# A windowed-attention transformer behind a state-space block on one core: scores and values in one alternating run, copies and waits in another order, and a new ending

## What is computed

```python
for i in range(6):
    # attention: 16 heads of 64, windows of 32, each looks at itself and the window before
    q, k, v = split(shift_tokens(x) @ Wqkv[i]);  q, k = l2norm(q) * qs, l2norm(k) * ks   # then rotary with scale
    sim  = where(mask, -inf, q @ k2.T * 8)        # 32 x 64 for each window and head
    x    = softmax(sim) @ v2 @ Wo[i] + x
    # feed-forward
    xn = layernorm(shift_tokens(x)) * g + b
    a, gate = split(xn @ W1[i] + b1[i]);  x = (a * gelu(gate)) @ W2[i] + b2[i] + x
out = resid + gb * x
```

## Time and profile before

| | us |
|---|---|
| median of 3 runs | 2083.33 |
| lowest and highest | 2079.34, 2084.64 |
| the profiled execution | 2082.23 |
| its span, first to last instruction | 2080.4 |
| busy: TensorE, VectorE, ScalarE, GpSimd | 1992.2, 1520.1, 1383.3, 1227.6 |
| mean granted share of TensorE's clock | 0.975 |

### The profile page before, as it was taken

The page is one execution under the profiler, slowest core; times in us unless marked ns, Lnnn a source line. Parts: engine busy times, 40 slices in busy tenths (PEclk is TensorE's granted clock), DMA queues, the critical chain, the costliest instruction groups (busy, mean ns, idle before and its releaser), DMA issues. The chain is left out here.

```text
span 2080.4 us, 82225 instructions
## 1 busy us (share of the span) xinstructions
PE 1992.2 (96%) x32996; PEld 1395.7 (67%) x32996; DVE 1520.1 (73%) x2879; ACT 1383.3 (66%) x4165; POOL 1227.6 (59%) x1376
## 2 busy tenths in 40 slices
PE   7788798999999999999999999999999999999987
PEld 3333233887687786876877868768768677687672
DVE  1499896886786776867867768679678687686763
ACT  4532233886786776867867777678678776686772
POOL 1376774775585564855756756559456566575550
PEclk9888888999999999999999999999999999999998
DMA  1421110311131111221111211112211111121110
GB/s 62 134 71 71 60 61 4 102 44 39 38 93 40 38 44 32 50 84 37 47 36 40 87 37 45 38 35 57 79 38 47 38 41 40 32 54 30 27 29 21
DMA packets 148091, 104.30 MB, mean 50 GB/s; under 512 B 15778, under 2 KB 140256, under 8 KB 146176
## 3 DMA queue, kind: packets, MB, share of 16 engines
q1 hardware_dynamic: 147712, 99.07, 17.1%
HBM read 48.31 MB, written 1.18 MB: 24 GB/s over the span
## 5 line engine op out<-in xcount | busy, mean ns | idle before, releaser
L1401 POOL TENSOR_TENSOR QK<-QK,RN 128x512 f32<-128x512 f32 x384 | 400.2, 1042 | 375.2 <-ACT RN L1134 360.1
L1144 ACT ACTIVATE PR<-ps,MN 128x64 f32<-128x64 f32 x1536 | 355.9, 315 | 155.6 <-DVE MN L1262 140.0
L1009 PE MATMUL ps<-W,XS 128*128 128x256 f32 x1536 | 434.9, 406 | 5.1 <-PEq L64 4.1
L1396 POOL TENSOR_TENSOR QK<-PC,PS 128x256 f32<-128x256 f32 x384 | 279.7, 728 | 247.8 <-PE ps L995 243.8
L1170 ACT COPY QKT<-ps 128x512 f32<-128x512 f32 x384 | 224.6, 585 | 245.9 <-PE ps L995 245.8
L1286 DVE TENSOR_REDUCE SS<-SQ 128x8 f32<-128x512 f32 x384 | 262.2, 683 | 57.6 <-ACT SQ L1177 55.6
L1009 PEld LDWEIGHTS ps<-W,XS 128*128 128x128 f32 x1536 | 260.8, 189 | 61.6 <-issue 4.9
L1397 POOL TENSOR_TENSOR QK<-PC,PS 128x256 f32<-128x256 f32 x384 | 280.8, 731 | 0.0
L1262 DVE TENSOR_REDUCE MN<-ps 128x4 f32<-128x256 f32 x384 | 162.9, 424 | 149.8 <-PE ps L957 148.1
L1305 DVE TENSOR_TENSOR PC<-ps,TC 128x512 f32<-128x512 f32 x384 | 261.2, 680 | 0.1
L1307 DVE TENSOR_TENSOR PS<-ps,TS 128x512 f32<-128x512 f32 x384 | 260.4, 678 | 0.0
(11 more groups left out here) (137 smaller groups left out, 3216.3 us busy)
## 6 DMA issues: line engine op xcount, KB each, us to landing
V<-V SPq DMA_DIRECT2D x384, 97.5 KB, 2.2
scr<-B_rows SPq DMA_DIRECT2D x32, 512.0 KB, 3.6
V<-V SPq DMA_DIRECT2D x288, 32.5 KB, 2.4
W<-in_Wqkv SPq DMA_DIRECT2D x40, 192.0 KB, 2.9
TC<-in_tcos SPq DMA_DIRECT2D x6, 1024.0 KB, 5.1
TS<-in_tsin SPq DMA_DIRECT2D x6, 1024.0 KB, 8.5
WO<-in_Wo SPq DMA_DIRECT2D x6, 512.0 KB, 4.1
W<-in_W SPq DMA_DIRECT2D x6, 341.0 KB
```

The source lines that it names most:

```text
L1009: mm = nc.tensor.matmul(ps[:, par, k * 2 * P:(k + 1) * 2 * P], cols[k], W[:, i, 0:2, :].rearrange("p t m -> p (t m)"), start=True, stop=True)
L1144: e = nc.scalar.activation(PR[:, m % 2, h, slot * DH:(slot + 1) * DH], ps[:, 3 + h, slot * DH:(slot + 1) * DH], ACT.Exp, scale=-1.0, bias= ...
L1396: nc.gpsimd.tensor_tensor(QK[:, par, :, 0:hd], PC[:, par, :, 0:hd], PS[:, par, :, hd:DH], ALU.add)
L1401: nc.gpsimd.tensor_tensor(QK[:, par, :, :], QK[:, par, :, :], bcast_last(RN[:, m // 2 % 2, 8 * par:8 * par + 8], DH), ALU.mult).then_inc(q ...
```

## The change

What it does, in six parts:

1. In a steady turn the 16 score products and the 16 value products are issued as one run, `scores_and_values(n)`. Score k is followed by value k-2, both taken from `spread_tiles`, so that neighbours in the run use different tiles. The last score product, which raises `s_ps`, is the 29th of 32. Turns before 8 and after 383 keep the two separate runs.
2. ScalarE copies v first (`copy_v`) and then the probabilities (`copy_p`), in all turns. In the feed-forward turn both stand between gates as before, exchanged.
3. In steady turns the wait for `prods` stands at the first mask product and no longer at the projection, and the wait for `v_cp` before the values is gone.
4. The drain has 8 turns. Ten of the 16 output products of the last pass (`early_wo`) are put between its turns, the other six between mean and variance.
5. The last pass's layer end (`t == LAST`) spreads over several PSUM banks, mixes gate and up products of both halves, and has its layer norm on VectorE (`last_norm`) in place of GpSimd.
6. The final scaling and sum are products: `out_rows` transposes the input XRES by the identity and adds XT times DG, a diagonal matrix with the batch's scale that GpSimd makes once. The 8 VectorE instructions of L1363 go, and the feed-forward sum of the last two passes is written to XT. The result is copied into XRES's memory and stored from there. Batch 0's rows are done while the last layer end is still running.

```diff
+        DG = sb("DG", [P, B, P])
+        OUT = XRES[:].rearrange("p (n m) -> p n m", m=D)
...
+        LAST = 2 * DEPTH - 1
+        DRAIN = NSTEPS + 8
+        early_wo = {1: [(0, 0), (0, 1)], 2: [(0, 2)], 3: [(0, 3)], 4: [(0, 4), (0, 5)], 5: [(0, 6)],
+                    6: [(0, 7), (1, 0), (1, 1)]}
...
+            def scores_and_values(n):
+                if not steady(n):
+                    return
+                for k in range(18):
+                    if k < 16:
+                        h, quad = spread_tiles[k % 8]
+                        mm = score(n - 5, k // 8, h, quad)
+                        if k == 15:
+                            mm.then_inc(s_ps, 1)
+                    if k >= 2:
+                        slot, quad = spread_tiles[(k - 2) % 8]
+                        mm = value(n - 7, (k - 2) // 8, slot, quad)
+                mm.then_inc(o_ps, 1)
...
                 for h in range(2):
+                    if steady(n) and h == 0:
+                        pe.wait_ge(prods, n - 1)
                     if steady(n) and h == 1:
                         pe.wait_ge(v_sh[(n - 7) % 4], 32 * ((n - 7) // 4 + 1))
                     nc.tensor.matmul(ps[:, 3 + h, 0:P], identb[:], MASKB[:, int(s == 0), h, :], start=True, stop=True)
                 if steady(n):
                     pe.wait_ge(pT, n - 6)
+                if steady(n):
+                    return
...
-                wait(pe, v_cp, min(n, NSTEPS))
+                    wait(pe, v_cp, min(n, NSTEPS))
...
-                wait(pe, prods, n - 1)
+                if not steady(n):
+                    wait(pe, prods, n - 1)
...
+            def out_pair(t, c, k):
+                mm = nc.tensor.matmul(ps[:, wo_bank(t, c), :], WO[:, k, :], OT[:, c, k, :], start=(k == 0),
+                                      stop=(k == PAIRS - 1), skip_group_check=True)
...
+            def out_rows(b, c, bank):
+                for k in range(4):
+                    cols = slice((2 * b + c) * CH + k * P, (2 * b + c) * CH + (k + 1) * P)
+                    nc.tensor.matmul(ps[:, bank, k * P:(k + 1) * P], XRES[:, cols], ident[:], start=True, stop=False)
+                    mm = nc.tensor.matmul(ps[:, bank, k * P:(k + 1) * P], XT[:, cols], DG[:, b, :], start=False, stop=True)
+                mm.then_inc(fT_ps, 1)
...
+                for c, k in early_wo.get(n - NSTEPS, ()):
+                    pe.wait_ge(oT, PHASE * LAST + 4 * k + 2 + 2 * c)
+                    out_pair(LAST, c, k)
...
                     copy_out(n)
                     squares(n)
+                    copy_v(n)
                     copy_p(n)
-                    copy_v(n)
...
-            for c in range(NCH):
-                dve.wait_ge(x2, 4 * DEPTH)
-                for half, x in x_halves(c // 2, c % 2):
-                    o = slice(c * CH, (c + 1) * CH)
-                    last = nc.vector.scalar_tensor_tensor(XT[half, o], x, MOD[half, 5, c // 2:c // 2 + 1],
-                                                          XRES[half, o], ALU.mult, ALU.add)
-                last.then_inc(fin, 1)
```

More of the change, by code:

```diff
@@ L1087, in feed_forward @@
                     pe.wait_ge(hid, 6 * t + 5 + c)
[L1088 to L1094, removed]
+                    w2_product(t, c)
+            def out_rows(b, c, bank):
[4 more added lines that the diff above has]
+                mm.then_inc(fT_ps, 1)
+            for n in range(DRAIN):
+                u, t = n % PHASE, n // PHASE - 1 if n < NSTEPS else -1
                 if u == U_FFN + 1 and t >= 0:
@@ L1112, in _ @@
                         feed_forward(t, n)
-            for c in range(NCH):
[L1115 to L1119, removed]
+                if n == NSTEPS + 1:
+                    pe.wait_ge(prods, NSTEPS)
+                for c, k in early_wo.get(n - NSTEPS, ()):
+                    pe.wait_ge(oT, PHASE * LAST + 4 * k + 2 + 2 * c)
+                    out_pair(LAST, c, k)
+            pe.wait_ge(x2, 2 * LAST)
+            mean(LAST, 0)
+            out_pair(LAST, 1, 2)
+            out_pair(LAST, 1, 3)
+            var(LAST, 0)
+            for k in (4, 5, 6):
+                out_pair(LAST, 1, k)
+            pe.wait_ge(oT, NSTEPS)
+            out_pair(LAST, 1, 7)
+            pe.wait_ge(s_dg, B)
+            for c in range(2):
+                out_rows(0, c, 3 + c)
+            pe.wait_ge(qkT, NSTEPS)
+            mean(LAST, 1)
+            pe.wait_ge(xg, 2 * LAST + 1)
+            pe.wait_ge(lnv, 2 * LAST + 1)
+            gate_product(LAST, 0)
+            gate_product(LAST, 1)
+            var(LAST, 1)
+            pe.wait_ge(fcp, 1)
+            gate_product(LAST, 2)
+            pe.wait_ge(fcp, 2)
+            up_product(LAST, 0)
+            pe.wait_ge(cen, 2 * LAST + 2)
+            up_product(LAST, 1)
+            pe.wait_ge(lnv, 2 * LAST + 2)
+            up_product(LAST, 2)
+            pe.wait_ge(xg, 2 * LAST + 2)
+            for k in range(3):
+                pe.wait_ge(gel, 6 * LAST + k + 1)
+                gate_product(LAST, 3 + k)
+            for k in range(3):
+                pe.wait_ge(hid, 6 * LAST + k + 1)
+                up_product(LAST, 3 + k)
+            pe.wait_ge(gel, 6 * LAST + 4)
+            w2_product(LAST, 0)
+            pe.wait_ge(gel, 6 * LAST + 5)
+            pe.wait_ge(hid, 6 * LAST + 6)
+            w2_product(LAST, 1)
+            for c in range(2):
+                pe.wait_ge(x2, 2 * LAST + c + 1)
+                if c == 0:
+                    pe.wait_ge(on, NSTEPS)
+                    pe.wait_ge(v_cp, NSTEPS)
+                    pe.wait_ge(pT, NSTEPS)
+                out_rows(1, c, 5 + c)
         @block.scalar
```

169 lines of the change are left out of this document (110 added, 59 removed).

## The result

The changed kernel takes 2202.0 us (median of 3 runs, 2201.3 to 2203.2), the kernel before 2083.3: 1.0575 times as long, interval 1.0551 to 1.0599. The profiled runs have spans of 2199.5 and 2080.4 us at granted clocks of 0.979 and 0.975, so the clock is not the reason.

The account below looks back on a forecast made before the run. TensorE, busy 96% of the span, was taken to bound the kernel at 3.28 us a step. Profiled 2082 + 87 (plain steps) + 6 (slow clamps) - 5 (covered steps) - 17 (ending) = 2153 us, range 2085 to 2215.

Parts of the forecast that it names:

- MN waits for score 16, held behind 13 values: Single run: VectorE's minimum (MN) waits for score 16, 29th of 32 products, which comes 0.26 us later.
- x: Time from the start of a scores run to the start of its last record: 0.24 us before, 0.50 forecast.
- t: The start of a scores run on TensorE, from which the forecast measures a step's times.
- plain steps: 299 attention steps without extra products or the old form: forecast 3.57 us in place of 3.28, +87 us.
- v first, chain x + 3.07: ScalarE's copies: probabilities end 0.27 us later, so the chain from scores to next scores becomes x + 3.07 = 3.57.
- `prods` at the mask, 40 slow clamps at 0.16: VectorE's chain at the mask: 3.73 us with slow norm clamps, 0.16 above ScalarE's, 40 times, +6 us.
- 77 covered steps gain 0.06 each: Steps whose extra feed-forward-pass products cover the delay: TensorE stays the bound, run 0.73 for 0.79 us, -5 us.
- The ending, -17: Last pass: 58.1 us from output projection to end becomes 35 after the drain plus 6 of drain growth, gain 17.
- TensorE's share falls to near 90%: Sign on the busy line: TensorE's share falls from 96% as it idles before the first score, about 0.35 a step.
- strict order on tiles: Rival in the single run: a product blocked on its tile holds all behind it, x 0.62 to 0.95, 2229; chance 0.10.
- Scores stay early: Rival in the single run: scores run ahead of values on their tiles, x 0.24 to 0.40, 2075 to 2123; chance 0.11.
- faster: Rival: run 0.06 shorter in all steps, both chains below 3.22, x below 0.24 or shorter ScalarE links, 2042; chance 0.11.

Follow-up runs that it names:

- the kernel with two runs: The changed kernel with 16 scores and then 16 values as separate runs, v's copy first and `prods` at the mask kept: 2099.2 us, 1.0081.
- values two tiles back: The changed kernel with each value on the tile used longest ago, `(k - 4) % 8` for `(k - 2) % 8`, score 16 still 29th: 2193.5 us, 1.0534.
- values 4 behind: The changed kernel with value k-4 behind score k in place of k-2, score 16 the 27th product: 2182.0 us, 1.0473.
- 8 behind: The changed kernel with value k-8 directly behind score k on the same tile, score 16 the 23rd product: 2170.5 us, 1.0421.

## Why the prediction was right, and where it was not

The forecast was 2153 with 2085 to 2215, slower; it is 2202. By its steps:

- *MN waits for score 16, held behind 13 values.* Right, and this is the 103 us. The size was off: x was to be 0.50, below the forecast's own 0.56 for each kind at its own pace; it is 0.66 by the last record, 0.60 by what MN sees of it (0.94 less the 0.34 of before). Each product put ahead of score 16 delays MN by 27 ns on average, where 0.50 had 20 in it. MN came 0.94 after t instead of 0.84, 299 x 0.10 = 30 us. Only 19 of them show in the plain steps (+112 against +93): in turns 11, 13, 14, 15 and 17 of a pass, where the kernel before was often above 3.28 already, the changed one is 0.27 longer on average, and not 0.40.
- *v first, chain x + 3.07.* Right: with 0.60 it gives 3.67. The links behind MN sum to 2.74, where those read off the kernel before, with the copies exchanged, gave 2.73. The wait before the first score was to be 0.35 a step and is 2.1 / 11 = 0.19, as TensorE's own turn had grown as well, to 3.59.
- *`prods` at the mask, 40 slow clamps at 0.16.* Right in kind and place, smaller in the changed kernel (2.4 us by the traces, not 6), and larger in the kernel with two runs.
- *77 covered steps gain 0.06 each.* Wrong, and it is the step that failed: they lose 22 us. Both ends of it were wrong. The run became longer, 0.91 and not 0.73, where it was 0.79 before; 77 x 0.12 = 9. And MN's delay goes on to ON, for which v's projection waits. From the first projection to the transposes of PR it now takes 1.60 in all of them; before it was 1.41 to 1.44 in five of the seven turns and 1.54 in turns 7 and 9. That is 1.0 a pass, 11 us. In turns 6, 12 and 16 the wait for PT adds 0.09, 3 us. Together these medians give 23. I had followed what the scores release through ScalarE and through PS, not through ON, which is the shortest way back to TensorE.
- *The ending, -17.* Right: -15 by the trace, -17 by the kernel with it alone. Behind the drain it is 35.3 where the forecast had 35, and the drain grew by 7.6 where 6 was counted.
- *TensorE's share falls to near 90%.* Wrong. It stayed at 96%: records are drawn past the start of the next, which covers waits of 0.1 to 0.2, and v's projection is drawn longer where it is held (L1068 0.71 in the step above, 0.61 in the earlier trace rows).

Of the rivals, *strict order on tiles* had the better number, 2229, and the wrong cause: its x of 0.62 to 0.95 comes from a tile's full turn between a score and its value, and with value directly behind score on one tile the kernel was faster, not slower. *Scores stay early* and *faster* asked for an x of 0.40 or less and 0.24 or less; it is 0.60. The Trainium skill ("TensorE: Matmul & The Clock Gate", Part 3, The mechanism) says that products start and end in program order. The trace does not agree for these small float32 products: ahead of the first value stand three scores in the program, six records, but 13 score records start before the first of L972. So scores do run ahead of values, only not far enough; the last one still starts at 0.66. With the values two tiles back it is the other way round, three score records and not six, as the rows in the last section show.

Not tried: v's projection behind the transposes of PR, which would give ON time. Why a product ahead of the last score costs 27 ns is open, and so is what sets the run's length: values 4 behind and values two tiles back have the same sequence of tiles but at the ends (in both a tile is used again after nine and seven places), and take 0.85 and 0.79.

## What to carry to other kernels

If one engine is full and two others wait at the head of what it releases, the place of the releasing instruction in its queue can be worth more than the length of the run: here a release that came 0.36 us later cost 0.28 a step against the kernel with two runs. Follow every result that the delayed instruction gates back to the full engine, the shortest way first. And don't look for such a loss in busy shares; divide the span by the steps, and read the waits of the weight loads. A run that is put together may be no shorter: here it was 0.12 longer, and at best as long as the two.

## What was not expected of the hardware

- Alternation of scores and values does not keep the two paces. Alone they start 15.5 and 24 ns a product; in two blocks the last value record starts 0.64 after t, in the changed kernel 0.77, two tiles back 0.65. MN comes 27 ns later, on average, for each product put ahead of the last score.
- The time from the first of 32 alternating products to the projection depends on the order of the tiles: 0.91 with the value five places behind the score on its tile, 0.85 at 4 behind, 0.87 directly behind, 0.79 two tiles back.
- By their starts, score records overtake values that stand ahead of them in the queue, on other tiles: 13 records before the first value in place of 6, and at 8 behind 23 in place of 18 (first rows). With the values two tiles back the first value takes a tile that none of the three scores ahead of it uses, and starts behind 3 records in place of 6 (second rows), 0.02 after t and not 0.14:

```profile
2086.43 0.45 PE L964 MATMUL ps<-QKT 64*32 64x64 f32 x23
2086.68 0.22 PE L972 MATMUL ps<-V,PT 64*32 64x65 f32 x1
```
```profile
2045.35 0.25 PE L964 MATMUL ps<-QKT 64*32 64x64 f32 x3
2045.37 0.24 PE L972 MATMUL ps<-V,PT 64*32 64x65 f32 x1
```

- A clamp of 128x16 on VectorE takes 0.16 us alone and up to 0.88 beside GpSimd. Each clamp of over 0.3 us in the twelve traces, 846 of them, starts while a GpSimd instruction runs and ends 26 to 36 ns after it.
